# Attention's output turned by TensorE instead of by transfers, FFN's low parts moved from VectorE to GpSimd, output bias from GpSimd to VectorE

## What is computed

```python
xn = layernorm(x)                       # x: 8 batches of 512 tokens x 256
q, k, v = xn @ wq + bq, xn @ wk + bk, xn @ wv + bv       # 16 heads of 16
q, k = rope(q), rope(k)
attn = softmax(q @ k.T / 4 + causal) @ v                 # by head
s = attn @ wo + bo
h = silu(xn @ wg.T) * (xn @ wu.T)                        # 768 wide
x = x + s * silu(h @ wd.T)                               # wg, wu, wd: int8 range / 127
```

## Time and profile before

| | |
|---|---|
| time, median of three runs | 553.73 us (550.44 to 556.63) |
| the profiled execution | 555.2 us |
| its span | 553.7 us |
| busy: PE, DVE, ACT, POOL | 480.0, 425.1, 330.0, 332.1 us |
| mean granted clock of TensorE | 0.95 |
| transfers | 76.65 MB, 138 GB/s |

### The profile page before, as it was taken

One profiled execution on the slowest core, in us unless ns is written; L12 is line 12 of the kernel. 1 busy time (PEld: TensorE's weight loads), 2 busy tenths in 40 slices (PEclk: granted clock), 3 DMA queues, 4 the chain that ended last, 5 costly groups with the idle time before them and its releaser, 6 DMA issues.

```text
span 553.7 us, 13804 instructions
## 1 busy us (share of the span) xinstructions
PE 480.0 (87%) x5397; PEld 367.7 (66%) x5397; DVE 425.1 (77%) x667; ACT 330.0 (60%) x683; POOL 332.1 (60%) x439
## 2 busy tenths in 40 slices
PE   0679899979989999998999988999999988889873
PEld 0466797857667766785778675777668666558633
DVE  3398879946898799978996798769987768875713
ACT  2663256645785666666666756655674756663670
...
GB/s 290 110 178 167 83 53 135 114 213 128 105 75 212 197 160 181 158 130 148 170 140 95 223 85 88 160 176 216 136 93 134 164 174 155 158 151 64 3 78 38
DMA packets 59667, 76.65 MB, mean 138 GB/s; under 512 B 15056, under 2 KB 30928, under 8 KB 59600
## 3 DMA queue, kind: packets, MB, share of 16 engines
...
HBM read 41.91 MB, written 29.82 MB: 130 GB/s over the span
## 4 chain that ended last, share of the span: by engine, by line
PE 38%; DVE 25%; DMA 13%; ACT 8%; issue 7%; SPq 6%; POOL 2%; DVEq 0%; ACTq 0%; POOLq 0%
PE ps_w L618 22%; DVE row_max L982 9%; PE ps_w L749 5%; DMA sum_rows<-o_t 5%; PE ps_w L647 4%; ACT probs L863 4%; PE ps_w L663 4%; DMA at_lo<-inv_rows 4%; DVE h_lo L434 3%; DVE hid L1028 2%; DVE hid L1023 2%; DVE attn L991 2%; PE ps_w L650 2%; DVE high_low L972 1%; SPq L549 1%
## 5 line engine op out<-in xcount | busy, mean ns | idle before, releaser
L982 DVE TENSOR_REDUCE row_max<-ps_w 128x2 f32<-128x1024 f32 (+3 forms) x256 | 199.7, 815 | 42.0 <-PE ps_w L650 41.6
L863 ACT ACTIVATE probs<-ps_w 128x512 f32<-128x512 f32 (+1 forms) x384 | 181.0, 535 | 78.1 <-PE ps_w L663 65.2
L1094 POOL TENSOR_SCALAR_AFFINE_SELECT probs<-probs 128x256 f32<-128x256 f32 x256 | 109.4, 449 | 123.1 <-ACT probs L863 122.9
L647 PE MATMUL ps_w<-k_st,q_st 48*128 48x512 f32 (+3 forms) x512 | 80.8, 355 | 19.5 <-DVE row_max L982 6.5
L663 PE MATMUL ps_w<-q_st,k_st 49*128 49x512 f32 (+3 forms) x512 | 78.8, 353 | 16.0 <-DMA q_st<-minus_max 5.8
L618 PE MATMUL ps_w<-xt_hi,wgu_hi 64*128 64x512 f32 x384 | 84.9, 430 | 3.0 <-DVE wgu_lo L961 1.3
L618 PE MATMUL ps_w<-xt_lo,wgu_hi 64*128 64x512 f32 x384 | 80.4, 407 | 0.0
L749 PE MATMUL ps_w<-probs,vals 128*32 128x512 f32 (+3 forms) x1024 | 79.1, 450 | 0.7 <-POOL probs L1094 0.4
L647 PEld LDWEIGHTS ps_w<-k_st,q_st 48*128 48x128 f32 x512 | 49.1, 195 | 39.8 <-issue 11.8
L663 PEld LDWEIGHTS ps_w<-q_st,k_st 49*128 49x128 f32 x512 | 47.2, 193 | 35.0 <-ACT probs L863 8.7
L749 PEld LDWEIGHTS ps_w<-probs,vals 128*32 128x32 f32 x1024 | 29.1, 112 | 41.0 <-issue 29.7
...
## 6 DMA issues: line engine op xcount, KB each, us to landing
...
```

The source lines that it names most:

```text
L647: pe.matmul(dst[h][:, col:col + (t + 1) * P], q_st[64 * h:64 * h + STACK, pair, t * P:(t + 1) * P], k_st[64 * h:64 * h + STACK, pair, 0:(t ...
L863: nc.scalar.activation(probs[:, (pair % 2) * SLOTS + slot, col:col + WIDTH[c]], w_of(kind, b, 3 * pair + c // 2, c % 2)[:, 0:WIDTH[c]], AC ...
L982: last = nc.vector.tensor_reduce(of_pair, both_of(kind, b, i)[:, :, col:col + (t + 1) * P], AX.X, ALU.max)
L1094: nc.gpsimd.affine_select(out=v, in_=v, compare_op=ALU.is_ge, fill=0.0, base=0, pattern=[[0, 2], [1, P]], channel_multiplier=-1).then_inc( ...
```

## The change

- `BY_PE` and the kinds `NA`, `NB`, `NC`, `ND`, `RC`, `AM` are gone: all eight batches take the way that batch 7 took. That adds to TensorE 28 `ON` and 14 `AT`, 8 transposes each, which take two PSUM banks each; to VectorE 28 `ON` of three instructions; the 14 pairs of high and low parts read PSUM instead of SBUF. It takes 196 transfers out of SyncE's list.
- `POOL_LOWS` names all six hidden tiles: the 48 low parts `HL` go from VectorE to GpSimd.
- The bias: `GB` (32 adds and products on GpSimd) and `BO` are gone. VectorE adds `bo_row`, in PSUM, to the output projection before the product (16 instructions).
- `ORDER` is another order throughout, with other banks.

```diff
-POOL_LOWS = ()
+POOL_LOWS = (0, 1, 2, 3, 4, 5)
...
         def add_x(eng, tensor_tensor, b, i):
             need(eng, prod_ready, 2 * b + i + 1)
-            need(eng, bias_added, 2 * b + i + 1)
+            if i == 0:
+                need(eng, res_in, 16 * (b + 1))
             r = res[:, 2 * i:2 * i + 2, :].rearrange("p t d -> p (t d)")
             tensor_tensor(r, r, gate[:, b % 2, i, :], ALU.add).then_inc(res_ready, 1)
...
-                elif kind == "NA":
-                    g, k = b * GROUPS + i, i // 2
-                    need(sp, o_t_ready, g + 1)
-                    need(sp, inv_stored[i % 2], 16 * (g // 2 - 1))
-                    sp.dma_start(sum_rows[i], o_t[HD:P:32, :]).then_inc(sums_stored, 16)
...
-                    raw = attn_of(k)[0]
-                    for hh in range(4):
-                        at = 64 * (i % 2) + HD * hh
-                        sp.dma_start(raw[at:at + HD, :], o_t[32 * hh:32 * hh + HD, :]).then_inc(raw_placed, 16)
...
-                    at = 64 * (i % 2)
-                    rows = inv_rows[i].rearrange("h (a c) -> h a c", a=1).broadcast_to([4, HD, SEQ])
-                    sp.dma_start(attn_of(k)[1][at:at + 64, :], rows).then_inc(inv_placed[k], 16)
...
                 elif kind == "AT":
-                    need(pe, attn_ready, (GROUPS // KT) * (i + 1))
+                    need(pe, attn_ready, b * GROUPS + (GROUPS // KT) * (i + 1))
...
                 elif kind == "PV":
-                    g = b * GROUPS + i
-                    need(act, pv_done, (g + 1) * TT)
-                    if g <= GROUPS * BY_PE:
-                        need(act, sums_stored, 16 * g)
-                        need(act, raw_placed, 64 * g)
+                    need(act, pv_done, (b * GROUPS + i + 1) * TT)
                     nc.scalar.copy(o_t[:, :], w_of(kind, b, i)).then_inc(o_t_ready, 1)
                 elif kind == "AT":
-                    if b < BY_PE:
-                        need(act, scaled, KT * b + i + 1)
-                        if b:
-                            need(act, prod_ready, 2 * b)
-                        nc.scalar.copy(at_hi[:, i, :], attn_of(i)[0]).then_inc(at_hi_ready, 1)
-                        return
...
-                elif kind == "RC":
-                    need(dve, sums_in[i % 2], 16 * ((b * GROUPS + i) // 2 + 1))
-                    nc.vector.reciprocal(sums[:, i % 2, :], sums[:, i % 2, :]).then_inc(inv_ready, 1)
-                elif kind == "AM":
-                    need(dve, inv_placed[i], 32 * (b + 1))
-                    need(dve, raw_placed, 64 * (b * GROUPS + 2 * i + 2))
-                    raw, inv = attn_of(i)
-                    nc.vector.tensor_tensor(raw, raw, inv, ALU.mult).then_inc(scaled, 1)
                 elif kind == "ON":
                     wait_full(dve, "dve", kind, b, i)
                     heads = both_of(kind, b, i)[:, :, 0:TT * 64].rearrange("p s (n c) -> p s n c", c=32)
                     g = b * GROUPS + i
-                    need(dve, attn_ready, i)
-                    need(dve, at_ready, KT * b)
+                    need(dve, attn_ready, g)
...
-                    if b < BY_PE:
-                        nc.vector.tensor_tensor(at_lo[:, i, :], attn_of(i)[0], at_hi[:, i, :].bitcast(F32), ALU.subtract).then_inc(at_ready, 1)
-                        return
...
                 elif kind == "OP":
                     wait_full(dve, "dve", kind, b, 0, i)
                     ps = w_of(kind, b, 0, i)
-                    need(dve, bias_added, 2 * b + i + 1)
+                    by_tile = lambda ap: ap.rearrange("p (a d) -> p a d", d=DM)
+                    if b == 0 and i == 0:
+                        dve.wait_ge(bias_in, 16 * 4)
+                    nc.vector.tensor_tensor(by_tile(ps[:, :]), by_tile(ps[:, :]), by_tile(bo_row[:]).broadcast_to([P, 2, DM]), ALU.add)\
+                        .then_inc(sum_ready, 1)
+                    need(dve, sum_ready, 2 * b + i + 1)
                     nc.vector.scalar_tensor_tensor(out=gate[:, b % 2, i, :], in0=ps[:, :], scalar=0.5 * WSCALE, in1=gate[:, b % 2, i, :],
                                                    op0=ALU.mult, op1=ALU.mult).then_inc(prod_ready, 1)
...
-                elif kind == "GB":
-                    if b == 0 and i == 0:
-                        pool.wait_ge(bo_scaled, 1)
-                    need(pool, silu_ready, 2 * b + i + 1)
-                    need(pool, *rope_t_used[-1])
-                    need(pool, bias_added, 2 * b + i)
-                    by_tile = lambda ap: ap.rearrange("p (a d) -> p a d", d=DM)
-                    nc.gpsimd.tensor_tensor(by_tile(rope_t[:]), by_tile(gate[:, b % 2, i, :]), by_tile(bo_row[:]).broadcast_to([P, 2, DM]), ALU.mult)\
-                        .then_inc(gate_biased, 1)
-                    need(pool, gate_biased, 2 * b + i + 1)
-                    if i == 0:
-                        need(pool, res_in, 16 * (b + 1))
-                    r = res[:, 2 * i:2 * i + 2, :].rearrange("p t d -> p (t d)")
-                    nc.gpsimd.tensor_tensor(r, r, rope_t[:], ALU.add).then_inc(bias_added, 1)
-                    rope_t_used.append((bias_added, 2 * b + i + 1))
```

275 lines of the change are left out of this document (120 added, 155 removed).

## The result

The changed kernel takes 530.03 us (median of 4, 529.5 to 534.63); the kernel before took 553.58 on the same chip. The medians here take every execution, while the ratios leave out those in a slower state and compare runs of one chip; the median of the kernel before was 552.1 to 557.6 us on the five chips used, so a difference of a few us between kernels of two chips is better read from their ratios.

What follows compares the result with a forecast made beforehand. TensorE's own work was taken to bound the kernel, VectorE second. Terms +18.9 (transposes) - 6.7 (VectorE waits) - 3.0 (`k_st` load) - 2.0 (clock) + 1.3 (end) = +8.5 us gave 562 us, 1.5% slower; range 547 to 574 us.

Steps and rivals of the forecast that it cites:

- 42 groups of transposes: On TensorE, 28 `ON` and 14 `AT` added at 0.45 us busy time each: +18.9 us.
- transfers: load of k_st, clock: Removing SyncE's 196 transfers brings the `k_st` load forward, 3.0 us, and recovers 2.0 us of TensorE clock; issuing otherwise mostly hidden.
- bias to VectorE, additions at the end: At the kernel's end, each of the last two products gets an addition ahead of it: 2 x 0.64 = +1.3 us.
- the sum is wrong at its root: Stated sign of failure: TensorE's busy time growing by much more or less than 19 us.
- the waits themselves are counted above: At the end of batches 5 and 6, transfer waits were held already counted, so only 2 us of clock was taken.
- The stall at 118 us: TensorE's idle around the `k_st` load, put down to transfers ahead of it on SyncE: 3.0 us gained, at most 5.3.
- The late clock: TensorE's granted clock of 0.88 from 440 to 510 us, tied to transfers: 2 us taken back, ends nothing and 8.4.
- VectorE's waits halved: TensorE's waits for VectorE where the pipeline is full, 13.5 us scaled, halved by a lighter VectorE: 6.7 us gained.
- My first rival: VectorE was the true limiter, late row maxima delaying other work; TensorE's idle falls below 16.6 us; 547 us, chance 0.20.
- GpSimd: Its 48 added low parts, each 0.43 us later, cost nothing, at most 20.6 us; rival of lateness 572 us, chance 0.07.
- The clock at the transposes: Rival: TensorE's clock falls at the new transposes, 24.5 us on top of 562, giving 586 us; chance 0.03.
- no case of its own: Another order of the lists shifts the time only a few us either way, inside the ranges; given no chance.

Runs made afterwards that it cites:

- a_double: Changed kernel with each transpose of `o_t` and `attn` issued twice, 48 more groups of eight on TensorE; 540.69 us, ratio 0.974.
- b_no_transfers: Kernel before, own order, without the attention's 196 transfers and the waits for them (stale numbers in batches 0 to 6); 538.39 us, ratio 0.967.
- a_lows_dve: Changed kernel, own order, with the 48 low parts of the FFN's activations back on VectorE; 545.42 us, ratio 0.985.
- b_no_lows: Kernel before, own order, with the FFN's 48 low parts left out (stale ones used), transfers and bias as before; 546.82 us, ratio 0.988.
- a_bias_pool2: Changed kernel with the bias back on GpSimd, its pairs placed 8.5 us behind the residual's load; 552.12 us, ratio 1.000.
- a_bias_pool: Changed kernel with the bias back on GpSimd, 4 us behind the residual's load or behind `DN` if later; 560.71 us, ratio 1.015.
- b_bias: Kernel before, own order, with only the bias moved from GpSimd to VectorE; 558.42 us, ratio 1.006.
- b_all2: Kernel before's order with all three parts of the change inserted and a second, better deal of PSUM banks; 585.69 us, ratio 1.056.
- b_pe: Kernel before, own order, with only the attention of batches 0 to 6 turned and scaled by TensorE and VectorE; 573.69 us, ratio 1.034.
- b_free_wait: Kernel before, own order, all 196 transfers kept but copying to places nothing reads, with no waits for their landing; 541.05 us, ratio 0.978.
- b_lows_bias: Kernel before, own order, with the FFN's low parts moved to GpSimd and the bias to VectorE, transfers kept; 565.59 us, ratio 1.018.
- b_nt_lows_bias: Kernel before, own order, without the attention's transfers, with the FFN's low parts on GpSimd and the bias on VectorE; 543.48 us, ratio 0.984.

## Why the prediction was wrong, point by point

The steps that failed: the transfers were priced from TensorE's rows alone, at 5.0 us, where their going gave 18.4; the transposes were charged their busy time, 18.9 us, where they add 9.3 or less; and the order of the lists was put at nothing, though it decides whether the parts pay. What each part measured:

| term | predicted | measured | by |
|---|---|---|---|
| 42 groups of transposes | +18.9 | +7.0 to +9.3 | a_double, new order |
| transfers: load of k_st, clock | -3.0 - 2.0 | -18.4 (12 to 24) | b_no_transfers, old order |
| lighter VectorE, by the low parts | -6.7 | -15.4, -6.8 | a_lows_dve, new order; b_no_lows, old order |
| bias to VectorE, additions at the end | +1.3 | -22 to -31; +3, not told from 0 | a_bias_pool2, a_bias_pool; b_bias, old order |
| order | 0 | not measured apart | |
| all | +8.5 | -23.6; +31 in the old order | result; b_all2 |

The measured parts don't add up, and shouldn't be added: +9.3 - 18.4 - 15.4 = -24.5 looks like the result, but only by choice of rows, since the bias in the new order would bring at least -22 more, and the same three parts in the old order cost 31 us. Each undoing in the new order also holds the misfit of what was put back. So the result is explained in its directions, and how it divides among the parts and the order stays open.

- **The transposes.** I took the group's busy time, 0.45 us, as its price. Right as a duration, wrong as a price: the next matmul starts before the group ends, and 0.22 us is what a group adds. That is 9.6 us or more of the 32 us by which I missed. Busy time of TensorE did not grow by 19 us, my own sign that the sum is wrong at its root.
- **The transfers.** Of the terms that were measured this one was furthest off. I wrote that issuing them is mostly hidden since TensorE waits little for transfers, and looked only at TensorE's rows. The row was in front of me: L986 and L991 of the earlier trace rows end with 14.7 and 4.8 us of idle time until a transfer landed. VectorE was blocked on top of its work: 425 + 19.5 = 445 us, which the change brings to 399.5. I counted the work and left out the 19.5 us of standing. Of these only 7.5 us lie in the middle, where VectorE is at 85%; 11.9 us lie from 440 to 510 us, and there my "the waits themselves are counted above" was wrong, for what was counted were TensorE's waits up to 440 us, scaled. Of the work, too, I counted too much: VectorE's busy time fell by 25.6 us, not 31.7. The rows of two groups can overlap (b_no_lows leaves out a group of 44.9 us, and the busy time falls by 38.2).
- **The stall at 118 us.** I gave the transfers 3.0 us there. b_no_transfers has the same stretch as before (62.78 busy, clock 0.90), so they do not make it. Nor does it need the new order to go: the clock of that stretch is 0.98 in b_no_lows, with all transfers, and in b_pe, with the low parts on VectorE. In the changed kernel it is gone too; what makes it was not settled.
- **The late clock.** The row was read rightly: from 440 to 510 us the clock goes from 0.88 to 0.98 in b_no_transfers, but only to 0.90 in b_free_wait. I took 2 us of at most 8.4; 0.10 x 70 = 7 us came back there. In the changed kernel it is 0.93 from 440 to 490 us.
- **VectorE's waits halved.** In the old order b_no_lows gives 6.8 us for the low parts, as I had said. That the two agree is luck in part: b_no_lows takes more off VectorE than the change does, and half of what its trace gains, 5.6 of 11.1 us, is there by 171 us, behind the stretch around 118 us that I had put down to the transfers. In the new order they give 15.4. I had taken the queue as fixed, and scaled the waits that the trace names. My first rival says that a late row maximum also delays the work that the trace puts down to ScalarE and transfers. Its point of decision, less than 16.6 us of idle time, was passed (14.0), so it came nearest. But VectorE's load alone is not the cause, since b_lows_bias has 27.5 us less of it and is 10 us slower by the ratio; and its 547 us were 17 too many, with the transposes at 18.9 and nothing for VectorE's standing.
- **GpSimd.** Costed at nothing, rightly in the new order: its trace has 3.0 us of waits of ScalarE's tanh for low parts, and none of TensorE for masks. In the old order the same move, with the bias to VectorE, costs some 10 us by the ratios (b_nt_lows_bias against b_no_transfers; b_lows_bias against before).
- **The clock at the transposes.** The middle stays at 0.99 with six more groups of a batch, and at 0.99 to 1.00 with twelve. The Trainium skill, "TensorE: Matmul & The Clock Gate", Part 4 on PE-mode transpose, says that a transpose doesn't count as TensorE being busy in the same way. If it holds here, such groups are gaps to the clock; no run here shows an effect of them, at groups this short among matmuls.
- **The order as "no case of its own".** Wrong: b_all2, with the same work in the old order, takes 586 us, 12 above the slow end of my range. The order and the banks decide whether the parts pay.
- **The end.** Each addition stands ahead of its product and takes 0.70 us, where I had taken 0.64; in order of time, one of the last two pairs:

```profile
520.46 0.70 DVE L947 TENSOR_TENSOR ps_w<-ps_w,bo_row 128x512 f32<-128x512 f32 x1 [3.61 <-PE ps_w L571]
521.19 0.69 DVE L950 SCALAR_TENSOR_TENSOR gate<-ps_w,gate 128x512 f32<-128x512 f32 x1
```
